# DLRM interaction and tower: fifteen tables looked up by products, 44 gathers, gram as 27x27 products on four column tiles

## The reference

```python
e = jnp.stack([tbl_0[ids[:, 0]], ..., tbl_25[ids[:, 25]]], axis=1)      # (512, 26, 128)
all_emb = jnp.concatenate([r_bottom_output[:, None, :], e], axis=1)     # (512, 27, 128)
gram = jnp.einsum('bfd,bgd->bfg', all_emb, all_emb)                     # (512, 27, 27)
z = gram[:, triu_i, triu_j]                                             # (512, 351)
h = jnp.concatenate([z, r_bottom_output], axis=1)                       # (512, 479)
h = jnp.maximum(h @ W_top1 + b_top1, 0.0)                               # 479 -> 512
h = jnp.maximum(h @ W_top2 + b_top2, 0.0)                               # 512 -> 256
y = h @ W_top3                                                          # 256 -> 1
```

## Time and profile before

| | us |
|---|---|
| median of 3 runs | 148.09 (147.55 to 148.1) |
| span of the profiled execution, slowest core | 148.2 |
| PE busy, PEld busy | 119.3, 102.7 |
| DVE busy, ACT busy, POOL busy | 68.2, 66.1, 75.1 |
| first gram product | 79.1 |

### The profile page before, as it was taken

How to read it: one execution, slowest core, us unless ns; L and a number is a source line. 1 busy time by engine, 2 the same in 40 slices (tenths; PEclk the granted TensorE clock), 3 DMA queues, 4 the chain that set the end, 5 groups by cost and what they waited for, 6 DMA issues and landing times.

```text
span 148.2 us, 1947 instructions
## 1 busy us (share of the span) xinstructions
PE 119.3 (80%) x714; PEld 102.7 (69%) x714; DVE 68.2 (46%) x141; ACT 66.1 (45%) x102; POOL 75.1 (51%) x77
## 2 busy tenths in 40 slices
PE   5729549884977097783946999999999999999993
PEld 5617337552745074661736999899799998998981
DVE  6065446464655090743300499775026901358110
ACT  3022060717181361706528494553946185364121
POOL 6777877878787777877777777720000000000000
PEclk9975855998699758699598699999999999999999
DMA  2444444644444447759454211210000000000000
GB/s 40 101 155 156 158 158 146 192 149 156 146 151 153 149 149 211 179 161 236 149 146 131 61 38 53 53 40 0 0 0 4 0 0 0 4 0 0 0 4 1
DMA packets 6477, 13.45 MB, mean 91 GB/s; under 512 B 1853, under 2 KB 2365, under 8 KB 6468
## 3 DMA queue, kind: packets, MB, share of 16 engines
q1 hardware_dynamic: 4228, 8.74, 18.6%
q0 software_dynamic: 2240, 4.59, 12.0%
HBM read 13.32 MB, written 0.00 MB: 90 GB/s over the span
## 4 chain that ended last, share of the span: by engine, by line
DMA 40%; PE 39%; DVE 8%; issue 7%; ACT 2%; SPq 1%; DVEq 0%; ACTq 0%
DMA raw<-tbl 22%; DMA ids_b<-ids_t 18%; PE gps L539 16%; PE ring L563 6%; PE ring L572 4%; PE ring L559 4%; PE ring L521 3%; PE ring L510 3%; DVE gram L426 2%; DVE onehot L408 2%; DVE lo L417 2%; PE ring L579 1%; DVE z L447 1%; ACT ids_f L295 1%; PE ring L547 1%
## 5 line engine op out<-in xcount | busy, mean ns | idle before, releaser
L282 POOL DMA_INDIRECT rows<-tbl,ids_sb x70 | 72.9, 1042 | 21.2 <-issue 21.2
L510 PE MATMUL ring<-onehot,hi 125*128 125x512 f32 (+1 forms) x72 | 26.7, 507 | 21.2 <-ACT hi L307 16.8
L510 PEld LDWEIGHTS ring<-onehot,hi 125*128 125x128 f32 x72 | 17.2, 258 | 27.3 <-issue 18.4
L539 PE MATMUL gps<-emb 128*123 128x108 f32 x256 | 30.4, 281 | 3.5 <-issue 3.2
L539 PEld LDWEIGHTS gps<-emb 128*123 128x123 f32 x256 | 29.6, 197 | 4.3 <-issue 4.0
L408 DVE TENSOR_SCALAR onehot<-ids_f 125x512 fp32r<-125x512 f32 (+1 forms) x72 | 25.6, 420 | 7.7 <-ACT ids_f L295 7.7
L426 DVE COPY gram<-gps 32x216 f32<-32x216 f32 x32 | 16.7, 523 | 22.8 <-PE gps L539 22.5
L307 ACT CAST hi<-raw 125x1024 fp32r<-125x1024 f32 (+1 forms) x9 | 9.0, 998 | 36.1 <-DMA raw<-tbl 24.1
L510 PE MATMUL ring<-onehot,lo 125*128 125x512 f32 (+1 forms) x72 | 24.3, 468 | 0.2
L417 DVE TENSOR_TENSOR lo<-raw,hi 125x1024 fp32r<-125x1024 f32 (+1 forms) x10 | 11.2, 1117 | 27.4 <-issue 22.7
L345 ACT COPY gram<-gps 32x216 f32<-32x216 f32 (+1 forms) x32 | 16.8, 527 | 13.5 <-PE gps L539 13.3
(11 more groups left out here) (29 smaller groups left out, 55.4 us busy)
## 6 DMA issues: line engine op xcount, KB each, us to landing
raw<-tbl SPq DMA_DIRECT2D x8, 500.0 KB
ids_b<-ids_t SPq DMA_DIRECT2D x9, 250.0 KB
rows<-tbl,ids_sb POOLq DMA_INDIRECT x70, 4.0
w1z<-w SPq DMA_DIRECT2D x1, 702.0 KB
w_sb<-w SPq DMA_DIRECT2D x1, 512.0 KB
raw<-tbl SPq DMA_DIRECT2D x2, 250.0 KB
bot<-bottom_t SPq DMA_DIRECT2D x1, 256.0 KB, 18.7
w1b<-w SPq DMA_DIRECT2D x1, 256.0 KB
```

Of the source, the lines that this page charges most:

```text
L282: nc.gpsimd.indirect_dma_start(out=rows[:, t, slot - 1, :], out_offset=None, in_=tables[table], in_offset=bass.IndirectOffsetOnAxis(ap=ids ...
L510: mm = nc.tensor.matmul(ring[:, b, 0:width], part_of[:, t % HL_RING, chunk * D:(chunk + 1) * D], onehot[:, n % OH_RING, k, 0:width], start ...
L539: mm = nc.tensor.matmul(gps[0:GM, n % 2, k, 0:Q * NF], four.rearrange("d q f -> d (q f)")[:, 0:GM], four[:, :, 0:NF], start=True, stop=True)
```

## The change

- Fifteen tables are looked up for all tiles, ten of 1,000 rows (eight chunks) and five of 1,250 rows (`LONG`, ten chunks); eleven are gathered, 44 indirect DMAs. Between two gathers GpSimd writes a memset of 128x32 and waits for it.
- Each table is loaded by two DMAs, partitions 0 to 111 and 112 to 124; ids are broadcast over 128 partitions, four buffers (`ID_RING`). `ids_sb` is loaded by ScalarE's queue.
- ids' difference to a partition's first row is `far` (three buffers), by ScalarE; table 0 is compared with ids themselves. In the order, the split of table j+2 stands behind the copy of look j, and `far` of table j+2 behind that (and behind a turn, where there is one).
- Gram: one 27x27 product a sample, its output at partitions 32q of a bank for q = 0 to 3, 512 products. A tile's 128 are four steps of 32, between which other steps stand. Two copies a tile bring them out, one by ScalarE, one by VectorE, each of 128x432.
- `emb` has 28 slots a sample in place of 32. Turns write PSUM in the order of `emb`.
- w1b x bottom is a step of its own ("bottom") ahead of l1, read from `bot`, in three banks of its own; the ring has two banks.
- 7 warm-up products in place of 12; the memsets of `emb` and `gram` are gone; y leaves in four DMAs.

```diff
-LOOKED_UP = [1, 2, 4, 16, 17, 18, 20, 21, 24]
-LOOK_FROM = [0, 0, 0, 0, 0, 0, 0, 0, 2]
+LOOKED_UP = [1, 2, 4, 8, 16, 17, 12, 18, 20, 13, 21, 24, 15, 25, 19]
+LONG = [8, 12, 13, 15, 19]
...
+    behind = {1: (0, 0), 3: (0, 1), 4: (0, 2), 6: (1, 0), 7: (1, 1), 8: (1, 2), 10: (2, 0), 12: (2, 1)}
+    order += [("compare", 0, 0)]
+    for j in range(NL):
+        if j + 1 < NL:
+            order.append(("compare", j + 1, 0))
+        order.append(("look", j, 0))
+        if j in behind:
+            order.append(("turn", *behind[j]))
+    order += [("gram", 0, 0), ("turn", 2, 2), ("turn", 3, 0), ("gram", 0, 1), ("bottom", 0, 0), ("turn", 3, 1),
+              ("gram", 0, 2), ("bottom", 0, 1), ("bottom", 1, 0), ("gram", 0, 3), ("turn", 3, 2), ("gram", 1, 0),
+              ("gram", 1, 1), ("pairs", 0, 0), ("l1", 0, 0), ("l1", 0, 1), ("gram", 1, 2), ("l1", 0, 2), ("l1", 0, 3),
...
 # SyncE
+            def load_rows(j, c0, c1, landed):
+                table = tables[LOOKED_UP[j]].rearrange("(p k) d -> p (k d)", k=chunks(j))
+                for p0, p1 in ((0, SPREAD), (SPREAD, KP)):
+                    sp.dma_start(raw[p0:p1, j % RAW_RING, c0 * D:c1 * D],
+                                 table[p0:p1, c0 * D:c1 * D]).then_inc(landed, 16)
...
 # GpSimd
+                        if n:
+                            nc.gpsimd.memset(idle[:], 0.0).then_inc(apart, 1)
+                            pool.wait_ge(apart, n)
                         nc.gpsimd.indirect_dma_start(
...
 # ScalarE
                 elif step == "look":
-                    if t and t + 1 < NL:
-                        float_ids(t + 1)
-                        split(t + 1)
                     act.wait_ge(oh_used, 2 * (t + 1))
+                    nc.scalar.copy(emb[:, :, :, slot_of(t)],
+                                   gps[:, t % GPS, :].rearrange("d (t p) -> d t p", t=TILES)
                                    ).then_inc(emb_look, 1)
+                    if t + HL_RING < NL:
+                        split(t + HL_RING)
...
 # TensorE
-                        for k in range(UNIT):
-                            four = emb[:, t, Q * (UNIT * n + k):Q * (UNIT * n + k + 1), :]
-                            mm = nc.tensor.matmul(gps[0:GM, n % 2, k, 0:Q * NF],
-                                                  four.rearrange("d q f -> d (q f)")[:, 0:GM],
-                                                  four[:, :, 0:NF], start=True, stop=True)
+                    for k in range(rest * STEP, (rest + 1) * STEP):
+                        for q in range(Q):
+                            one = emb[:, t, Q * (UNIT * unit + k) + q, 0:NF]
+                            mm = nc.tensor.matmul(gps[QP * q:QP * q + NF, gram_bank(t, unit), k * NF:(k + 1) * NF],
+                                                  one, one, start=True, stop=True)
```

More of the change, by code:

```diff
@@ L75, with chunks @@
 M1, M2 = H1 // 128, H2 // 128
-GM = (Q - 1) * QP + NF
-UNIT = 8
+UNIT = 16
 UNITS = U // UNIT
-BANKS = 4
-WARM_UP = 12
-OH_RING = 3
+STEPS = 4
+STEP = U // STEPS
+BANKS = 2
+GPS = 3
+TOP = 3
+WARM_UP = 7
+OH_RING = 4
 HL_RING = 2
 RAW_RING = 3
+ID_RING = 4
+FAR_RING = 3
 def slot_of(j):
-    return 1 + ORDERED.index(LOOKED_UP[j])
-def turns_until(t, g):
-    return sum(len(GROUPS[x]) for x in range(t)) + g + 1
+    return 1 + NG + j
+def chunks(j):
+    return KCS[1] if LOOKED_UP[j] in LONG else KCS[0]
@@ L96, in work_order, with row_column @@
+def row_column(j, c):
+    return (KCS[0] if LOOKED_UP[j] in LONG else 0) + c
 def work_order():
-    turns = [("turn", t, g) for t in range(TILES) for g in range(len(GROUPS[t]))]
     order = []
[L101 to L111, removed]
@@ L115, in work_order @@
[L115 to L126, removed]
@@ L133, in work_order, with gram_bank, turn_count @@
     return order
 ORDER = work_order()
-USES = [use for use in ORDER if use[0] not in ("compare", "gram")]
+USES = [s for s in ORDER if s[0] in ("turn", "pairs", "l2", "l3")]
 def bank(step, i, part=0):
     return USES.index((step, i, part)) % BANKS
+def gram_bank(t, unit):
+    return (UNITS * t + unit) % GPS
+def turn_count(t, g):
+    return TURNS * t + g + 1
 def tower(nc, bottom, ids, ids_t, tables, w1, b1, w2, b2, w3, out):
@@ L288, in _, with split @@
         def _(act):
[L289 to L304 removed]
+            def split(j, half=0):
@@ L305, in split @@
                 if j >= HL_RING:
                     act.wait_ge(oh_used, 2 * (j - HL_RING + 1))
-                nc.scalar.copy(hi[:, j % HL_RING, start:], raw[:, j % RAW_RING, start:]).then_inc(hi_ready, halves)
-            for step, t, part in ORDER:
-                if step == "compare":
-                    if t == 0:
-                        for j in range(HL_RING):
-                            float_ids(j)
-                            split(j)
+                if j == 0:
+                    each = chunks(0) // 2 * D
+                    act.wait_ge(raw_in[0] if half else first_raw_in, 32)
+                    part = slice(half * each, (half + 1) * each)
+                    nc.scalar.copy(hi[:, 0, part], raw[:, 0, part]).then_inc(hi_ready, 1)
+                    return
@@ new lines, in split @@
+                act.wait_ge(raw_in[j % RAW_RING], 32 * (j // RAW_RING + 1))
+                nc.scalar.copy(hi[:, j % HL_RING, 0:chunks(j) * D], raw[:, j % RAW_RING, 0:chunks(j) * D]
+                               ).then_inc(hi_ready, 2)
+            act.dma_start(ids_sb[:], ids).then_inc(ids_in, 16)
+            act.wait_ge(row_ready, 2)
+            nc.scalar.activation(scrap[:], neg_row[:, 0:1], ACT.Relu)
+            for step, t, part in ORDER:
+                if step == "compare" and t == 0:
+                    split(0, 0)
+                    split(0, 1)
+                elif step == "compare":
+                    act.wait_ge(idb_in[t % ID_RING], 16 * (t // ID_RING + 1))
+                    if t > FAR_RING:
+                        act.wait_ge(oh_dve, 2 * (t - FAR_RING + 1))
+                    c = row_column(t, 0)
+                    nc.scalar.activation(far[:, t % FAR_RING, :], ids_b[0:KP, t % ID_RING, :], ACT.Identity,
+                                         bias=neg_row[:, c:c + 1]).then_inc(far_ready, 1)
+                    if t < HL_RING:
+                        split(t)
@@ L420, in _ @@
+                        ins.then_inc(oh_dve, 1)
+                        if half == 0 and t > 0:
+                            rest(t, 0, chunks(t) * D, 2)
+                    if t == 0:
+                        rest(0, 0, chunks(0) // 2 * D, 1)
+                        rest(0, chunks(0) // 2 * D, chunks(0) * D, 1)
                 elif step == "gram":
+                    if part != STEPS - 1:
+                        continue
                     if t >= 2:
                         dve.wait_ge(pairs_ready, 2 * (t - 1))
[L423 to L430 removed]
```

341 lines of the change are left out of this document (156 added, 185 removed), and 4 rows, old and new, of the table behind.

## The result

The changed kernel takes 140.5 us (median of 4 runs, 139.46 to 140.92), the kernel before on the same chip 148.09 (4 runs, 147.55 to 149.98): a ratio of 0.9487, 95% interval 0.9434 to 0.954. The forecast was 139.2, in a range of 122 to 154. The profiled execution took 140.92 us, its span 139.2.

The account below looks back on a forecast made before the run. The prediction saw two stages: 79 us feeding lookups, with 125-partition transfers using about five of 16 DMA engines, then 69 us of TensorE. Its sum was 82.4 + 26.0 + 5.8 + 25.0 = 139.2 us, range 122 to 154.

Parts of the forecast that it names:

- Term 1, the supply: Table loads: the split spreads transfers over all 16 engines, 3.0 us a short table and 3.5 a long one.
- above 180: Total in us if the split does not spread the transfers, at 7.8 us a table; chance under 2%.
- Term 2, the loop: Lookups: copy, split, far, compares, subtract and products take 8.5 us for two short tables; gram starts at 82.4 us.
- Term 3, gathers: 44 gathers at 1.6 us each, over at 74 us and landed at 78, hidden before the last turn needs them.
- the cover of 1.9: Gathers: the period in us at which they stop being hidden.
- The rival of starving gathers: Gathers slowed beside VectorE's compares: at a 2.2 us period total 149, at 2.0 142; chance 12%.
- Term 4, gram: Gram's 1024 records of load and product cost by their columns, 0.0244 us each, 25.0 us in all.
- the 8 kept above: Gram: 8 us for full drains at some 30 switches between tiled and full array, taken as 0 in the sum.
- The dear-product rival: Gram: load and product of thin records run one after another, 50 us, total 164; chance 15%, from 0.033 us a record.
- Term 5, the rest: TensorE's work besides gram after 82.4 us: 26.0 us of records plus 5.8 us idle.
- The tiled rival: Gram products of four samples overlap, 6 to 10 us; VectorE's chain shows, +4; total 125; chance 20%.
- The rival of the looser loop: Lookups: ScalarE keeps ahead and VectorE alone binds, 73 us to gram, total 131; chance 8%.

Follow-up runs that it names:

- the run with four samples: The change with gram in products of four samples as before, 128 products, and a memset of emb's 28th slot added: 146.2 us.
- the last version: The change with far ahead, gram(1,1) moved behind the first half of l1, and the memset only before the first 22 gathers: 144.05 us.
- the combined version: The change with far of table j+2 ahead of look j and gram(1,1) moved behind the first half of l1: 139.0 us.

## Why the prediction was right, and where not

- **Term 1, the supply:** right. The share went to 0.7 to 1.0, SyncE's queue left the chain but for the first ids, and undoing the split alone costs 18 to 22 us. The rival's price ("above 180") is for tables and ids together, which no run undid.
- **Term 2, the loop:** right in its mechanism (moving `far` gave 5.2 us) and 5.0 us short, gram at 87.4 and not 82.4. Of this the first table is 3.1 (its copy at 15.1, not 12.0), the loop (5.08 - 4.95) x 14 = 1.8. The 12.0 is 4.8 sooner than the 16.8 of before, while the data were to come 3 to 4 sooner. They did, by 3.0 (first product at 7.38, not 10.36), but its 16 products took 7.7 us and not 6.4, 1.0 of it in a wait for `lo`, which VectorE makes behind all eight compares. Turn copies cost 0.72, not 0.8.
- **Term 3, gathers:** right. Period 1.69 against 1.6, under the cover of 1.9. The rival of starving gathers did not decide.
- **Term 4, gram:** the step that failed. The 24.4 ns of "a record costs its columns" come near on one tile (27 to 28 ns); four tiles run together 2.8-fold. The rival that said so had 20%, at 6 to 10 us for gram; it took 11 to 13. Where tiled and full products alternate the forecast took 0. From a full record to a gram record 0.20 us pass in the change and 0.11 in the run with four samples, at 13 places: some 1.2 us, far under the 8 kept above. The dear-product rival is excluded: 10.3 ns is under a third of its 33, and a sixth of the 62 ns that the Trainium skill's "TensorE: Matmul & The Clock Gate", section "Back-to-back issue gap", gives for decoding in software. The same page of the Trainium skill, "TensorE: Matmul & The Clock Gate", says in its part on packing small matmuls that products at different tile positions run concurrently; the runs agree, and it deserved more than the row of full-width products.
- **Term 5, the rest:** the second step that failed. 31.8 us had only 5.8 of idle time, and TensorE's own instructions had no place in the sum. They stop it wherever thin products are dense, VectorE's chain then shows, and the clock falls: 7 to 9 us. Of these the two stops are 3.5 (0.85 and 2.61, 0.6 of it VectorE's z), the twelve records at the low clock 1.3 (2.93 against 1.60), the entries into gram 1.2; the rest is not assigned. The tiled rival had priced the exposed chain at 4.
- The sum: +5.0, -12 to -14, +7 to +9. The number came out by luck, because two mis-sized terms had opposite signs, and not independently: the sooner gram is done, the more of the rest is uncovered.
- The rival of the looser loop says 131; its own terms give 139.2 - (82.4 - 73) = 129.8.
- By its own list, the prediction called itself wrong at gram records outside 15 to 33 ns and at a granted clock under 1.00 behind 85 us. Both happened.

What stays open is what the engines wait for in the standstill. Shown is that gathers are issued during all of it and that the long wait ends with the last; shorter ones follow. That it needs gathers in close succession is only argued: for it speak the change, untouched, and the last version with its short standstill; against it that the kernel without memsets had none, and that with `far` ahead gram crawled beside spaced gathers. Why the kernel before ran in 148 us in the result's session, with the same 70 gathers, isn't known. As for a faster version: the one with `far` ahead is the only one whose runs all lie under the change's, barely (137.37 at most against 137.65 at least; the medians differ by 2.7%), but the two weren't run on one chip; the combined version, which was, isn't told apart from the change.

## What to carry to other kernels

Count a transfer's partitions: 125 in one DMA cost 18 to 22 us here against 112 and 13. Thin products spread over four column tiles ran 2.8 times faster, but 256 instructions are then gone in 1.3 us: put wide work between them, and let nothing that others wait for stand right behind a dense run. When one stage becomes cheap, price the stage that it used to cover; and have the gathers over before the dense stage begins.

## Hardware behaviour that was not expected

- TensorE's instructions came in packets of 256, about 3.5 to 3.9 us apart where it drained them; between them it stopped for 0.8 to 2 us, and went on 1.2 to 1.5 us after a packet was in.
- While gathers were issued every 1.25 us, TensorE stood still for 26 us in one kernel, and in another ScalarE waited 33 us, the last 15 of them without work on TensorE and VectorE either (one profile each, on two chips). The kernel of 148 us took 176 to 200 in three sessions; the one profile of it there has this standstill.
- A gather held for 5.42 us and landings of 7.2 us at the median appeared when the pause between gathers was taken away.
